# A routed mixture kernel: who brings each tile's first expert weights, and how SyncE's token loads are written

## The reference, cut to what matters

```python
# gelu mixture, F = 512
logits = (x @ gate_w + gate_b) / TEMP            # top 2 of 8 are kept
h = gelu(einsum('bsd,edf->bsef', x, w1) + b1)
expert_out = einsum('bsef,efd->bsed', h, w2) + b2
out = einsum('bse,bsed->bsd', gate_probs, expert_out)   # then a layer norm
# swiglu mixture, I = 256: silu(x @ w1[e].T) * (x @ w3[e].T), times w2[e]
```

## Time and profile before

| what | us |
| --- | --- |
| median of three runs (1335.67 to 1336.85) | 1336.54 |
| span of the profiled execution, first to last instruction | 1697.2 |
| PE busy in that span | 1114.7 |
| DVE busy | 765.2 |
| ACT busy | 553.5 |
| POOL busy | 751.0 |

### The profile page before, as it was taken

How to read it: one execution, slowest core, us unless ns; L and a number is a source line. 1 busy time by engine, 2 the same in 40 slices (tenths; PEclk the granted TensorE clock), 3 DMA queues, 4 the chain that set the end, 5 groups by cost and what they waited for, 6 DMA issues and landing times. The chain is left out here.

```text
span 1697.2 us, 28236 instructions
## 1 busy us (share of the span) xinstructions
PE 1114.7 (66%) x6835; PEld 926.2 (55%) x6836; DVE 765.2 (45%) x2839; ACT 553.5 (33%) x1653; POOL 751.0 (44%) x802
## 2 busy tenths in 40 slices
PE   2376888437656699867477548289799734768482
PEld 2375888434346588757376547234344334657372
DVE  5221324158671133544146313269979762335132
ACT  1133546247413255533032113134343301223131
POOL 3634263521054625545715552255645456442522
PEclk9787999678966799978688769589999955879696
DMA  8544567310023345544354436100000003445363
GB/s 251 169 143 138 183 197 245 109 41 1 0 81 111 130 165 196 181 133 139 109 198 159 140 118 205 53 0 1 1 0 0 0 29 127 165 152 203 117 208 106
DMA packets 198792, 199.71 MB, mean 118 GB/s; under 512 B 22212, under 2 KB 140310, under 8 KB 198678
## 3 DMA queue, kind: packets, MB, share of 16 engines
q1 hardware_dynamic: 123138, 136.22, 23.5%
q0 software_dynamic: 16384, 33.59, 6.6%
q10 hardware_dynamic: 59156, 28.57, 5.9%
HBM read 52.44 MB, written 49.02 MB: 60 GB/s over the span
## 5 line engine op out<-in xcount | busy, mean ns | idle before, releaser
L611 PE MATMUL gelu_hb<-gelu_xsT,gelu_weights 128*128 128x128 f32 x2208 | 340.1, 298 | 65.5 <-issue 61.3
L611 PEld LDWEIGHTS gelu_hb<-gelu_xsT,gelu_weights 128*128 128x128 f32 x2208 | 308.7, 213 | 75.4 <-issue 73.5
L708 ACT ACTIVATE gelu_hid<-gelu_hb,gelu_weights 128x128 f32<-128x128 f32 x736 | 208.8, 374 | 238.6 <-remote 127.1
L1190 POOL DMA_INDIRECT slots_x<-gelu_xn,gelu_index x176 | 172.4, 980 | 203.6 <-DVE gelu_index L921 154.2
L622 PE MATMUL gelu_ob<-w,gelu_hid 128*128 x1472 | 220.0, 292 | 43.8 <-issue 41.5
L961 DVE TENSOR_TENSOR gelu_ys<-gelu_ob,bias 128x128 f32<-128x128 f32 x184 | 51.7, 291 | 392.4 <-PE gelu_ob L622 176.1
L622 PEld LDWEIGHTS gelu_ob<-w,gelu_hid 128*128 128x128 f32 x1472 | 198.7, 206 | 51.4 <-issue 51.1
L611 PE MATMUL swiglu_hb<-swiglu_xsT,swiglu_weights 128*128 128x128 f32 x736 | 114.8, 302 | 27.3 <-issue 27.2
L611 PEld LDWEIGHTS swiglu_hb<-swiglu_xsT,swiglu_weights 128*128 128x128 f32 x736 | 104.2, 217 | 29.0 <-issue 29.0
L952 DVE TENSOR_TENSOR gelu_hid<-gelu_sil,gelu_hb 128x256 f32<-128x256 f32 x92 | 38.4, 419 | 151.9 <-ACT gelu_sil L712 82.0
L952 DVE TENSOR_TENSOR swiglu_hid<-swiglu_sil,swiglu_hb 128x256 f32<-128x256 f32 x92 | 38.5, 419 | 149.3 <-ACT swiglu_sil L712 72.8
(11 more groups left out here) (375 smaller groups left out, 1997.1 us busy)
## 6 DMA issues: line engine op xcount, KB each, us to landing
gelu_weights<-w SPq DMA_DIRECT2D x184, 258.0 KB
gelu_weights<-s SPq DMA_DIRECT2D x92, 256.0 KB
swiglu_weights<-s SPq DMA_DIRECT2D x92, 256.0 KB
gelu_xs<-slots_x SPq DMA_DIRECT2D x69, 256.0 KB
slots_y<-gelu_ys ACTq DMA_DIRECT2D x138, 128.0 KB
swiglu_xs<-slots_x SPq DMA_DIRECT2D x23, 256.0 KB
slots_y<-swiglu_ys ACTq DMA_DIRECT2D x46, 128.0 KB
slots_x<-zeros SPq DMA_DIRECT2D x2, 1984.0 KB
```

Of the source, the lines that this page charges most:

```text
L611: last = pe.matmul(hb[j][:, c * P:(c + 1) * P], weights[:, j, c * P:(c + 1) * P], xsT[j // SET][:, j % SET, :], start=True, stop=True)
L708: last = act.activation(hid[:, j % RING, c * P:(c + 1) * P], hb[j][:, c * P:(c + 1) * P], ACT.Gelu, bias=weights[:, j, FF + c:FF + c + 1])
L1190: pool.indirect_dma_start(slots_x[:, :], bass.IndirectOffsetOnAxis(index[p][:, k, g:g + 1], 0), tokens[p][:, g, :], None).then_inc(sent[p] ...
```

## The change

The fills go from SP's DMAs to DVE. `weights` has eight slots in place of four (`HELD`); in iteration i DVE copies the weights of iteration i+1's four tiles, one copy ahead of each tile's own work, into the half of the ring that iteration i does not use. It reads the words itself: two per iteration, or three for two iterations in a hardware loop. The first four copies stand in the head of each mixture, behind `table(0)` and `stats(2)` and ahead of `route(1)`. The four semaphores `weights_ready` become one count, `weights_copied`.

SP keeps the token loads alone, each written out with a constant address and constant waits. The buffer `sil` is gone: ACT writes silu to `hid` and DVE multiplies in place, so ACT's silu now waits for `out_ready` where DVE's product did. In gelu0 the wait for the loaded tables is split: DVE waits for `w1` and its bias before its first copy, PE for `w2`. `back_small` of gelu0 lies over `s2`, to make room.

```diff
         def _(sp):
...
-            def fill(j, e, kind):
-                sp.dma_start(weights[:, j, 0:WIDTH[kind]], table_of[kind][:, bass.ds(e, 1), :].rearrange("p a f -> p (a f)")).then_inc(weights_ready[j], 16)
...
-            def body(i, stages, needs=None, loads=True):
-                now, fills, loading = stages
-                experts = experts_of(i + 1)
-                for j in range(BODY):
-                    sp.wait_ge(used_of[kinds[now]], i * BODY + (j + 1 + BANKS))
-                    sp.sem_inc(held, 1)
-                    fill(j, experts[j], kinds[fills])
+            def body(i, stage, needs=None):
                 if needs:
                     sp.wait_ge(sent[needs], SENT[needs])
-                    sp.wait_ge(table_ready, needs + 1)
-                if loads:
-                    sp.wait_ge(turned, i * 2 + 2)
-                    sp.wait_ge(loaded, i * 16 + 32)
-                    sp.sem_inc(held, 1)
-                    load(i + 2, loading)
+                sp.wait_ge(turned, i * 2 + 2)
+                sp.wait_ge(loaded, i * 16 + 32)
+                sp.sem_inc(held, 1)
+                load(i + 2, stage)
...
         def _(pe):
...
-                pe.wait_ge(weights_ready[j], i * 16 + 16)
+                pe.wait_ge(weights_copied, s + 1)
...
         def _(act):
...
+                act.wait_ge(out_ready, s + 1)
...
-                    act.activation(sil[:, j, :], hb[j][:, 0:FI], ACT.Silu).then_inc(sil_ready, 1)
+                    act.activation(hid[:, j % RING, 0:FI], hb[j][:, 0:FI], ACT.Silu).then_inc(sil_ready, 1)
...
         def _(dve):
...
+            def fill(slot, e, kind):
+                dve.tensor_copy(weights[:, slot, 0:WIDTH[kind]], table_of[kind][:, bass.ds(e, 1), :].rearrange("p a f -> p (a f)"))\
+                   .then_inc(weights_copied, 1)
...
+            def body(i, first, last, beside, ready, now, was, then):
+                word, u, odd = ready
+                ahead = None if last else [expert_in(word[u + 1], LAG + j) for j in range(BODY)]
                 for j in range(BODY):
                     s = i * BODY + j
+                    if not last:
+                        if not first:
+                            dve.wait_ge(hid_ready if was == "gelu" else h_ready, s + 1)
+                            dve.sem_inc(held, 1)
+                        fill((1 - odd) * BODY + j, ahead[j], then)
                     if now == "swiglu":
                         multiply(s, j)
```

More of the change, by code:

```diff
@@ L338, in mixture @@
     BANKS = BODY
+    HELD = 2 * BODY
     DIGITS = UNROLL * BODY
@@ L466, in mixture, with run @@
         group = lambda t, p: t[:, COL0[p]:COL0[p] + PART_GROUPS[p]]
-        def run(eng, body, beside, breaks=(), prepare=lambda i, needed: None):
+        def run(eng, body, beside, breaks=(), prepare=lambda i, turns: None):
             i = 0
@@ L624, in second_products, with word_of @@
                 last.then_inc(out_ready, 1)
-            def word_of(i, _needed):
+            def word_of(i, _turns):
                 return pe.value_load(words[0:1, bass.ds(i, 1)], min_val=0, max_val=E ** DIGITS - 1)
-            def body(i, first, last, beside, ready, now, was):
+            def body(i, first, last, beside, ready, now, was, then):
                 word, u, odd = ready
@@ L733, in copy_tokens, with body @@
                 act.copy(xT[:, n % XT, :], early[p][q][:, :]).then_inc(xt_copied, 1)
-            def body(i, first, last, beside, _ready, now, was):
+            def body(i, first, last, beside, ready, now, was, then):
+                _, _u, odd = ready
                 for j in range(BODY):
@@ L978, in body @@
                     if j % SET == SET - 1 and not (first and j < LAG):
-                        output(i * 2 + j // SET - 1, (j // SET + 1) % 2, i if j >= LAG else i - 1,
-                               experts[u * BODY + j - SET + 1:u * BODY + j + 1], now if j >= LAG else was)
+                        kind = now if j >= LAG else was
+                        es = [expert_in(word[u], j - SET + 1 + n) for n in range(SET)] if kind == "gelu" else None
+                        output(i * 2 + j // SET - 1, (j // SET + 1) % 2, i if j >= LAG else i - 1, es, kind)
                     for part in beside.get(j, []):
@@ L983, in body @@
                 if last:
-                    output(NTILES // SET - 1, 1, ITERS - 1, experts[BODY:BODY + SET], now)
+                    es = [expert_in(word[u], BODY + n) for n in range(SET)] if now == "gelu" else None
+                    output(NTILES // SET - 1, 1, ITERS - 1, es, now)
             def await_table(p):
@@ L1053, in _ @@
             stats(2)
+            dve.wait_ge(table_ready, 1)
+            if first_in:
+                dve.wait_ge(first_in, 32)
+            dve.sem_inc(held, 1)
+            word = word_at(0)
+            for j in range(BODY):
+                fill(j, expert_in(word, LAG + j), kinds[0])
             route(1)
@@ L1130, in _ @@
                 beside[20] = {1: at(later_weights["spreads"], dve)}
-            with_words = [p for p in range(1, min(NPARTS, PARTS + 1))] if gelu else []
-            run(dve, body, beside, {upto(p): (lambda p=p: await_table(p)) for p in with_words}, experts_of)
+            run(dve, body, beside, {upto(p) - 1: (lambda p=p: await_table(p)) for p in range(1, NPARTS)}, words_of)
             if both:
```

98 lines of the change are left out of this document (40 added, 58 removed).

## The result

The changed kernel takes 1344.26 us (median of four runs, 1343.17 to 1347.17) against 1336.11 us for the kernel before: 1.0059 of it, with a 95% interval from 1.0041 to 1.0078. It is 8 us slower, where I had forecast 18 us less.

A forecast was written before the change was run, and what follows sets the result against it. No engine filled the span; PE was busiest, with some 160 us of real stalls in the loops. -45 + 14 + 7 + 6 = -18 against 1336.5 gave 1318 us, the sum's own range 1295 to 1340.

The forecast's parts named there:

- The late token load (-45): Tile loops: PE's transposes wait for token loads issued behind the fills; earlier issue removes 29.2 to 85.5 us, taken as -45.
- the sign that I had named: Profile after: transposes' waits for the token loads near 0 where instructions run at their pace.
- The copies (+14 and +7): DVE's copies: hidden in plain iterations; about 15 swiglu iterations with routing work pay 14 us, plus 7 of the 45 not coming.
- the four of the earlier trace: Four swiglu iterations with routing work, lasting 8.4, 8.7, 7.9 and 6.8 us, forecast 0.9 us longer on average.
- The heads (+6): Head of each mixture: four copies and a read, 2.4 us, ahead of `route(1)` delay part 1's indices and scatters; +6 us.
- GpSimd held up: DVE's copies lengthen GpSimd's scatters, 79 us of POOL at worst, a third on the path: +26, 1344 us; chance 0.10.
- VectorE as the bound: Iterations with routing work: 20 pay 2.9 us whole, 58, heads 6, gain elsewhere 35: +29, 1366 us; chance 0.20.
- More comes back: Stalls are mostly late tokens and fills from q1's traffic: all 85.5 us go, 15 come, 1266 us; chance 0.18.
- The share that I gave to a gain: Chance that the changed kernel is faster: 0.59, against 0.11 within 0.2% and 0.30 slower.
- The slow stretches: Places in the earlier trace's loops where every engine's instruction crawls: some 361 us, taken as that profiled execution's own.
- a good quarter: Of 56.3 us of transposes' waits ending on "issue", 16 us counted as going, the rest placed in the slow stretches.

The follow-up runs named there:

- Thin fills: Kernel before, with each fill DMA after a mixture's first four moving 1 of 128 partitions (weights stale): 0.9848 of the kernel before, 1313.55 us.
- the fresh trace: Kernel before, unchanged, profiled again on a chip like that of the runs: time 1338.29 us, span 1336.5.
- the head-last version: Changed kernel with copies behind product and output, unused word not read in swiglu iterations, first copies behind places(1): 0.9955 of the kernel before, 1329.97 us.

## Why the prediction was wrong

**The late token load (-45).** This step failed. It read waits of 45 us out of the trace and counted every microsecond of them as time. Waits of 42 us went, but the stretches where they went, the 72 iterations without much routing work, gave 18.8 us, where the forecast had 38 for them (45 less the 7 set aside). Thin fills, which take away 22 us of the waits and leave the rest of the kernel as it was, give 20 us. Part of the difference can be seen: 4.4 us lay ahead of a point that GpSimd sets, in iteration 17, where TensorE only arrived earlier, and 6.3 us of wait went at iteration 58 only because TensorE arrived there later. Where the rest went was not followed. Of the waits left, 36.7 us are four that end on the DMA, in iterations 2, 25, 50 and 58 where a part's tokens begin, so the sign that I had named, token waits near 0, held elsewhere. The cause that I named was half of the true one. The load's late place costs nothing once the fills are gone. I had excluded the other half, the fills' traffic and issue, by saying that "the fills' own DMAs landed in time wherever an iteration has no gap". That holds for the fills. It says nothing of the token load behind them.

**The copies (+14 and +7).** Right in place, too small in size. The 7 us were a share of the 45 that wouldn't come, so the 14 us alone stand against the 21.5 us that the 17 iterations took more. For the four of the earlier trace rows I had 0.9 us more on average. In the fresh trace they take 8.2, 8.6, 7.6 and 7.0 us before and 10.4, 9.8, 9.3 and 7.7 after, 1.5 more. What I lacked is the price behind them, the lower clock of the iterations that follow (3.9 us in the two measured). Plain iterations stayed at 7.6 and 5.8 us, as forecast. These two rows after answer to the earlier trace rows:

```profile
1280.70:1286.50 5.80, 5.80 (x53) 5.80 (x53) 3.81 (x10) 2.16 (x6) 4.59 (x6) 1.00 0.49 136
161.40:169.00 7.60, 7.60 (x70) 7.60 (x69) 4.14 (x12) 6.51 (x25) 3.25 (x3) 1.00 0.29 82
```

The copy takes 427 to 430 ns at the median, under the 0.48 that I took. That the two reads of a word "mostly fall into the time in which silu isn't ready" was wrong where it mattered: dropping one of them was the best single edit.

**The heads (+6).** The size agrees with the run, 6 us back when the copies moved behind `route(1)`; the place is shown only in part. The first head costs 3.5 us up to iteration 3 (38.7 to 42.2 us from the first tile), and that comes back only when the copies stand behind `places(1)` too (39.3). The three iterations at the mixtures' ends and starts take 6.4 us more in the trace after, but 1.4 to 4.0 more in five other versions with the same heads, and 7.3 more in the head-last version, which is the fastest of all that keep the results right.

So the forecast's -38 + 14 + 6 = -18 came out as -18.8 + 21.5 + 6.4 = +9.1 in the traces and +8 in the runs. The first term is off by 19 us, the second by 7.5. The range missed the measured time by 4 us; its bounds, 29 us gone and 35 come, would give 1342.5.

**The rivals.** GpSimd held up was forecast at 1344 us, and the time was 1344.26, but that is luck: its work grew by 14 to 18 us, not by the 79 at worst. The Trainium skill, SBUF — State Buffer, section "SBUF: two separate sides", gives the 3100 ns for a DMA whose descriptors GpSimd writes beside a `tensor_copy`, and has GpSimd blocked until that copy ends. My estimate of 2.5 us for each meeting forgot that a copy here lasts 0.43 us, so that by the page no meeting could cost that much. The trace shows far less than my estimate, 27 ns on average; the longest of the 256 scatters took 1.62 us after and 1.50 us before. VectorE as the bound was the right mechanism, with prices too high on both sides: 58 us in the iterations with routing work against 21.5, and 35 us gained elsewhere against 18.8. More comes back named a true cause, the traffic in q1; it fell because the traffic was worth 20 us, and the 85 that it counted were waits, not time. The share that I gave to a gain rested on the first term alone.

**The slow stretches.** To set the sum against the runs and to leave the 361 us out was right for the runs' chip. But I read the split of the waits, a good quarter of those that end on "issue", out of a trace in which that split can't be seen.

## What to carry to other kernels

- A wait that can be named is not yet time. Follow its engine to the next point that another engine sets, here GpSimd's scatters and gathers: what is gained ahead of that point ends there.
- Before a wait for a DMA is put down to its late issue alone, ask what stands ahead of it. Three runs price it: the neighbour's bytes taken away (20 us less), the lateness put back without the neighbour (0 us), and the load moved ahead of the neighbour (its waits 36 us less, the time 1.2% more).
- On an engine that others wait for, work with slack belongs behind the work without, and a register read of 0.50 us counts as much as a copy of 0.43: 17 iterations went from 145.0 to 131.1 us with all copies still there.

## What the runs showed of the hardware

Two of the chips ran this kernel at 1692 and 1685 us in place of 1336, with every kernel slow at much the same iterations (4, 5, 21, 24, 27, 61, 70, 77, 84 and 90 among them). There the instructions themselves come late. Weight loads of the changed kernel at iteration 5 on such a chip, each started 0.7 or 1.4 us after the one before, with nothing to wait for:

```profile
134.84 0.19 PEld L584 LDWEIGHTS gelu_hb<-gelu_xsT,gelu_weights 128*128 128x128 f32 x1 [0.54 <-issue]
136.26 0.19 PEld L584 LDWEIGHTS gelu_hb<-gelu_xsT,gelu_weights 128*128 128x128 f32 x1 [1.23 <-issue]
```

The places are those of the trace before the prediction, whose iterations 4 and 5, with the earlier trace rows in them, are 35 us longer than in the fresh trace. So the slow stretches belong to places of the program on such chips. What is late there was not measured. The change is worth 2.8% on them and costs 0.6% on the others, so a comparison of two kernels has to say on which kind of chip it was made.
